# Expert projections of sorted rows: gated rows turned for two tiles at once, down projections on the two halves of the partitions

## The reference

```
xn = layernorm(x)
s  = attention(xn) @ w_out.T
expert = argmax(xn @ gate_w.T)                   # one of 8 for each of 4096 rows
inter  = relu(xn @ wg[expert])**2 * (xn @ wu[expert])   # 64 wide
g  = silu(inter @ wd[expert])                    # 256 wide
out = x + s * g
```

## Time and profile before

| | before |
|---|---|
| median of 3 runs | 1484.09 us |
| the profiled execution | 1485.04 us |
| its span | 1483.3 us |
| TensorE matmul busy | 1450.7 us |
| DVE busy | 1346.4 us |
| ACT busy | 1192.4 us |
| POOL busy | 162.1 us |
| bytes moved by DMA | 119.55 MB |

### The profile page before, as it was taken

The page is one execution under the profiler, slowest core; times in us unless marked ns, Lnnn a source line. Parts: engine busy times, 40 slices in busy tenths (PEclk is TensorE's granted clock), DMA queues, the critical chain, the costliest instruction groups (busy, mean ns, idle before and its releaser), DMA issues.

```text
span 1483.3 us, 31996 instructions
## 1 busy us (share of the span) xinstructions
PE 1450.7 (98%) x11197; PEld 652.2 (44%) x11197; DVE 1346.4 (91%) x1979; ACT 1192.4 (80%) x2381; POOL 162.1 (11%) x221
## 2 busy tenths in 40 slices
PE   7999999999999999999999999999999999999988
PEld 5555444434475433343434344434444444434326
DVE  6689999999846999999999999999999999999906
ACT  3653588888867888888888888888888888888890
POOL 5433322200001222000010000000010000000110
PEclk9999999999999999999999999999999999999999
DMA  5875244436263455333332342333323433333323
GB/s 186 277 204 137 65 84 83 76 46 125 39 188 90 80 111 99 52 48 48 48 44 41 48 99 42 46 46 48 48 44 45 97 48 41 48 48 48 69 70 117
DMA packets 79801, 119.55 MB, mean 81 GB/s; under 512 B 28962, under 2 KB 66210, under 8 KB 72738
## 3 DMA queue, kind: packets, MB, share of 16 engines
q1 hardware_dynamic: 73714, 105.82, 36.0%
q0 software_dynamic: 3072, 8.39, 2.2%
q10 hardware_dynamic: 2896, 3.62, 0.7%
HBM read 77.15 MB, written 39.71 MB: 79 GB/s over the span
## 4 chain that ended last, share of the span: by engine, by line
PE 94%; ACT 3%; DVE 1%; issue 1%; DMA 1%; SPq 0%; POOL 0%; ACTq 0%; POOLq 0%
PE ps L1243 39%; PE ps L1257 36%; PE ps L1231 5%; PE ps L1159 3%; ACT arena L658 2%; PE ps L1437 2%; PE ps L1160 1%; PE ps L1390 1%; PE ps L1374 1%; PE ps L1192 1%; PE ps L1184 1%; PE ps L1171 1%; PE ps L1341 1%; ACT x_sb L658 1%; PE ps L1136 0%
## 5 line engine op out<-in xcount | busy, mean ns | idle before, releaser
L1231 PE MATMUL ps<-ks,qs 48*128 48x512 f32 x1984 | 692.7, 444 | 0.0
L1243 PE MATMUL ps<-qs,ks 50*128 50x512 f32 x2048 | 680.6, 435 | 9.3 <-ACT x_sb L658 7.6
L809 DVE TENSOR_REDUCE arena<-ps 128x1 f32<-128x512 f32 x992 | 639.0, 681 | 16.5 <-PE ps L1231 16.2
L658 ACT ACTIVATE arena<-ps 128x512 f32<-128x512 f32 x1056 | 564.3, 605 | 86.9 <-PE ps L1243 79.7
L812 DVE TENSOR_REDUCE arena<-ps 128x1 f32<-128x1024 f32 x496 | 603.7, 1217 | 0.8 <-PE ps L1231 0.7
L658 ACT ACTIVATE x_sb<-ps 128x512 f32<-128x512 f32 x992 | 535.3, 598 | 64.9 <-PE ps L1243 44.9
L1243 PEld LDWEIGHTS ps<-qs,ks 50*128 50x128 f32 x2048 | 329.5, 184 | 485.0 <-issue 200.9
L1231 PEld LDWEIGHTS ps<-ks,qs 48*128 48x128 f32 x1984 | 325.2, 184 | 16.5 <-DVE arena L809 9.3
L1257 PE MATMUL ps<-arena 128*32 128x256 f32 (+1 forms) x3104 | 308.5, 469 | 5.5 <-ACT arena L658 4.1
L1257 PE MATMUL ps<-x_sb,arena 128*32 128x256 f32 (+1 forms) x2960 | 290.2, 464 | 0.0
L1257 PEld LDWEIGHTS ps<-arena 128*32 128x32 f32 x3104 | 62.3, 108 | 125.6 <-issue 125.6
(11 more groups left out here) (116 smaller groups left out, 623.2 us busy)
## 6 DMA issues: line engine op xcount, KB each, us to landing
qs<-parts_d SPq DMA_DIRECT2D x186, 128.0 KB
ks<-parts_d SPq DMA_DIRECT2D x186, 128.0 KB
parts_d<-arena SPq DMA_DIRECT2D x64, 256.0 KB, 2.8
xs_d<-arena SPq DMA_DIRECT2D x13, 384.0 KB, 3.5
arena<-xs_d SPq DMA_DIRECT2D x13, 384.0 KB, 3.8
ys_d<-arena SPq DMA_DIRECT2D x13, 384.0 KB, 2.8
x_sb<-in_x SPq DMA_DIRECT2D x2, 2048.0 KB, 13.1
onum_d<-arena SPq DMA_DIRECT2D x124, 32.0 KB
```

Of the source, the lines that this page charges most:

```text
L658: nc.scalar.activation(prob_of(pi, s, kb)[:, c * W:(c + 1) * W], ps[:, bank, :], ACT.Exp, scale=SCALE).then_inc(exp_done[bank], 1)
L809: nc.vector.tensor_reduce(most[head_slot][:, tile, u:u + 1], ps[:, AB + lo, :], AX.X, ALU.max).then_inc(a_reduced[u], 1)
L1231: ins = nc.tensor.matmul(ps[:, AB + c, :], qs[head_slot][ABASE:ABASE + KR, tile * P:(tile + 1) * P].bitcast(F32R), ks[head_slot][ABASE:ABA ...
L1243: nc.tensor.matmul(ps[:, bank, :], ks[s][at:at + KS, kb * P:(kb + 1) * P].bitcast(F32R), qs[s][at:at + KS, c * W:(c + 1) * W].bitcast(F32R ...
```

## The change

A step of each `experts` function now deals with a pair of tiles. The gated rows of an even tile go to columns 0 to 63 of `inter`, those of the odd tile behind it to columns 64 to 127. One turn makes both the stationary operand: the even tile on partitions 0 to 63 of `interT`, the odd tile on 64 to 127. The down projection of the even tile runs on partitions 0 to 63, that of the odd one on 64 to 127, one behind the other in TensorE's order and into banks 6 and 7. The down weights are loaded into both halves of `wd2` (four transfers, no longer two). The even tile takes them there, by the number of its expert; for the odd tile POOL copies the weights of its expert from the upper half of `wd2` to one of two fixed places in the tile `turn`, which is no longer used by then (`stage_down`). The zeroing by POOL goes. ACT does the copies and Relus of two tiles and then two Silus. SP's order of loads and stores is as before.

```diff
     NE = -(-NF // FP) * FP
+    NF2 = -(-NF // 2)
...
         res_at = at[0]
+        down_up = [turn[:, i * 8:(i + 1) * 8, :].rearrange("p t w -> p (t w)") for i in range(2)]
...
                                      src[:, k, :].rearrange("p (e f) -> p e f", f=DE)).then_inc(expert_weights, 16)
-                for i in range(2):
-                    sp.dma_start(wd2[0:DE, :, :].rearrange("p (c i) d -> p c i d", i=2)[:, :, i, :],
-                                 wd_in[i * DE:(i + 1) * DE, :, :]).then_inc(expert_weights, 16)
+                for half in range(2):
+                    for i in range(2):
+                        rows = wd2[half * DE:(half + 1) * DE, :, :].rearrange("p (c i) d -> p c i d", i=2)
+                        sp.dma_start(rows[:, :, i, :], wd_in[i * DE:(i + 1) * DE, :, :]).then_inc(expert_weights, 16)
...
                 sums_out(1, FB - 1)
-                for i in range(NF + 2):
-                    if i + 1 < NF:
-                        turned_out(i + 1)
-                    if i < NF:
-                        act.wait_ge(hid_done, i + 1)
-                        if i >= 2:
-                            act.wait_ge(inter_ready, i - 1)
-                        nc.scalar.activation(hr[i % 2], ps[:, EB + i % 2, 0:DE], ACT.Relu).then_inc(relu_done, 1)
-                    if i >= 2:
-                        act.wait_ge(y_done, i - 1)
-                        g, z = divmod(i - 2, FG)
-                        if g >= XR and z == 0:
-                            act.wait_ge(y_stored[g % XR], g // XR * 16)
-                        nc.scalar.activation(ysb[g % XR][:, z, :], ps[:, YB + i % 2, 0:D], ACT.Silu).then_inc(y_out, 1)
+                for j in range(NF2 + 2):
+                    for i in (2 * j, 2 * j + 1):
+                        if i + 1 < NF:
+                            turned_out(i + 1)
+                        if i < NF:
+                            act.wait_ge(hid_done, i + 1)
+                            if i >= 2:
+                                act.wait_ge(inter_ready, i - 1)
+                            nc.scalar.activation(hr[i % 2], ps[:, EB + i % 2, 0:DE], ACT.Relu).then_inc(relu_done, 1)
+                    for i in (2 * j - 4, 2 * j - 3):
+                        if 0 <= i < NF:
+                            act.wait_ge(y_done, i + 1)
+                            g, z = divmod(i, FG)
+                            if g >= XR and z == 0:
+                                act.wait_ge(y_stored[g % XR], g // XR * 16)
+                            nc.scalar.activation(ysb[g % XR][:, z, :], ps[:, YB + i % 2, 0:D], ACT.Silu).then_inc(y_out, 1)
...
-                for i in range(NF + 1):
-                    if i < NF:
+                for j in range(NF2 + 1):
+                    for i in (2 * j, 2 * j + 1):
+                        if i >= NF:
+                            continue
                         dve.wait_ge(relu_done, i + 1)
                         nc.vector.tensor_tensor(hu[i % 2], hr[i % 2], ps[:, EB + i % 2, DE:2 * DE], ALU.mult).then_inc(hu_ready, 1)
                         dve.wait_ge(hu_ready, i + 1)
-                        if i == 0:
-                            dve.wait_ge(pads_zeroed, 3)
-                        if i >= 2:
-                            dve.wait_ge(inter_turned, i - 1)
-                        nc.vector.tensor_tensor(inter[i % 2][:, 0:DE], hu[i % 2], hr[i % 2],
+                        if j >= 2:
+                            dve.wait_ge(inter_turned, j - 1)
+                        nc.vector.tensor_tensor(inter[j % 2][:, i % 2 * DE:(i % 2 + 1) * DE], hu[i % 2], hr[i % 2],
                                                 ALU.mult).then_inc(inter_ready, 1)
-                    if i >= 1:
-                        dve.wait_ge(inter_turned, i)
-                        if i >= 3:
-                            dve.wait_ge(y_done, i - 2)
-                        nc.vector.tensor_copy(interT[(i - 1) % 2], ps[:, PVB, 0:P]).then_inc(inter_out, 1)
+                    if j >= 1:
+                        dve.wait_ge(inter_turned, j)
+                        if j >= 3:
+                            dve.wait_ge(y_done, 2 * (j - 2))
+                        nc.vector.tensor_copy(interT[(j - 1) % 2], ps[:, PVB, 0:P]).then_inc(inter_out, 1)
...
+            def stage_down():
+
+                pool.wait_ge(expert_ready, 1)
+                pool.wait_ge(expert_weights, 16 * 8)
+                pool.wait_ge(v_staged[1], FB + 1)
+                for i in range(1, NF, 2):
+                    g, z = divmod(i, FP)
+                    if z == 1:
+                        packed = pool.value_load(expert[0:1, g:g + 1], min_val=0, max_val=E ** FP - 1)
+                    which = pool.snap(packed // E ** z % E, min_val=0, max_val=E - 1)
+                    if i >= 4:
+                        pool.wait_ge(y_done, i - 3)
+                    if i > 1:
+                        pool.wait_ge(down_staged, i // 2)
+                    nc.gpsimd.tensor_copy(down_up[i // 2 % 2][DE:P, :].unsqueeze(1),
+                                          wd2[DE:P, bass.ds(which, 1), :]).then_inc(down_staged, 1)
+
...
             pool.wait_ge(pt_out, NT)
-            nc.gpsimd.memset(wd2[DE:P, :, :], 0.0).then_inc(pads_zeroed, 1)
-            pool.wait_ge(pads_zeroed, 2)
-            for i in range(2):
-                ins = nc.gpsimd.memset(inter[i][:, DE:P], 0.0)
-            ins.then_inc(pads_zeroed, 1)
-            pool.wait_ge(pads_zeroed, 3)
             for pi in range(2, FB):
                 for s in range(2):
                     stage(0, pi, s, pi)
             for s in range(2):
                 stage(0, FB, s, FB)
+            stage_down()
...
-                pe.wait_ge(expert_weights, 16 * 6)
-                pe.wait_ge(pads_zeroed, 3)
-                for i in range(NF + 2):
-                    if i + 1 < NF:
-                        turn_sorted(i + 1)
-                    if i < NF:
-                        pe.wait_ge(xs_out, i + 1)
-                        if i >= 2:
-                            pe.wait_ge(relu_done, i - 1)
-                            pe.wait_ge(hu_ready, i - 1)
-                        for k in range(KC):
-                            last = nc.tensor.matmul(ps[:, EB + i % 2, 0:2 * DE], xsT[i % 2][:, k, :],
-                                                    wgu[:, k, bass.ds(which[i], 1), :], start=(k == 0), stop=(k == KC - 1))
-                        last.then_inc(hid_done, 1)
-                    if 1 <= i <= NF:
-                        if i == 1:
+                pe.wait_ge(expert_weights, 16 * 8)
+                for j in range(NF2 + 2):
+                    for i in (2 * j, 2 * j + 1):
+                        if i + 1 < NF:
+                            turn_sorted(i + 1)
+                        if i < NF:
+                            pe.wait_ge(xs_out, i + 1)
+                            if i >= 2:
+                                pe.wait_ge(relu_done, i - 1)
+                                pe.wait_ge(hu_ready, i - 1)
+                            for k in range(KC):
+                                last = nc.tensor.matmul(ps[:, EB + i % 2, 0:2 * DE], xsT[i % 2][:, k, :],
+                                                        wgu[:, k, bass.ds(which[i], 1), :], start=(k == 0), stop=(k == KC - 1))
+                            last.then_inc(hid_done, 1)
+                        if i + 1 < NF:
+                            expert_of(i + 1)
+                    if 1 <= j <= NF2:
+                        if j == 1:
                             pe.wait_ge(o_out[1], past(FB))
-                        pe.wait_ge(inter_ready, i)
-                        if i >= 2:
-                            pe.wait_ge(inter_out, i - 1)
-                        nc.tensor.transpose(ps[:, PVB, 0:P], inter[(i - 1) % 2], ident[:]).then_inc(inter_turned, 1)
-                    if i >= 2:
-                        if i == 2:
+                        pe.wait_ge(inter_ready, min(2 * j, NF))
+                        if j >= 2:
+                            pe.wait_ge(inter_out, j - 1)
+                        nc.tensor.transpose(ps[:, PVB, 0:P], inter[(j - 1) % 2], ident[:]).then_inc(inter_turned, 1)
+                    if j >= 2:
+                        if j == 2:
                             pe.wait_ge(a_reduced[GROUP_OF[YB - AB]], past(FB * 2 * KB + AHEAD - KB))
-                        pe.wait_ge(inter_out, i - 1)
-                        if i >= 4:
-                            pe.wait_ge(y_out, i - 3)
-                        nc.tensor.matmul(ps[:, YB + i % 2, 0:D], interT[(i - 2) % 2], wd2[:, bass.ds(which.pop(i - 2), 1), :],
-                                         start=True, stop=True).then_inc(y_done, 1)
-                    if i + 1 < NF:
-                        expert_of(i + 1)
-                pe.wait_ge(inter_out, NF)
+                        else:
+                            pe.wait_ge(y_out, 2 * (j - 2))
+                        pe.wait_ge(inter_out, j - 1)
```

(13 more changed lines are left out.)

## The result

The changed kernel takes 1497.90 us in the median of 6 runs (1491.03 to 1504.89), the kernel before 1483.74 (1482.64 to 1485.97): a ratio of 1.0087, with an interval of 1.0055 to 1.012. In a second set of runs it was 1496.92 against 1484.40, 1.0085 (1.0069 to 1.0101). It is slower by some 13 us, outside the range that was given; and its runs lie much wider apart than those of the kernel before in this set. (In larger sets that kernel has single long runs too, up to 1492.55 us at a mean clock of 0.993, where most of its runs have 0.997 or 0.998.) The profiled execution, of 1491.41 us, is one of the two shortest of its six.

The account below looks back on a forecast made before the run. It took SP's loads queued behind stores as decisive, 8.82 us per three steps, with ACT's 2.60 us a pair elsewhere. The stage ends at 458.0 instead of 456.19; 1.8 added to 1484.09 gives 1485.9 us, range 1480.5 to 1491.

Parts of the forecast that it names:

- The sum of the stage: Step times added over the experts' stage: last down pass at 458.0 instead of 456.19, 1.8 us slower.
- the clock: Rival, chance 0.20: clock halves inside the experts' stage, 0.75 us per 3.5 us stretch; seven such stretches give 1491.
- the rivals: Other cases: loads don't bind 0.17 (1481.4), clock falls 0.20 (1491), halves serial or sequencer overhead 0.12, POOL late 0.03.
- What bounds the kernel: In the experts' stage before the change, TensorE's own order sets the pace, 1.41 us a tile, and ACT follows.
- SP's chain: Loads of sorted rows queue behind stores awaiting Silus: every second group late, three steps 8.82 us; taken as decisive.
- ACT's chain: Two Silus in a row delay the copy that frees the turns' bank: 2.60 us a pair, 1.30 a tile.
- Counting the steps: Adding up ends of down passes through the experts' stage, from 405.3 to 458.0 for the last.
- Step 5: Pass 5 of TensorE's new pair loop, which waits for a load; its down passes were forecast to end at 414.65.
- step 2: Pass 2 of TensorE's new pair loop, where the count starts; about 1.1 us a tile without Silus, end at 405.3.
- The halves side by side: A pair's two down projections on TensorE run together, saving 0.38 of a possible 0.43 us a pair.
- The switch between the shapes: Row groups change TensorE's array shape twice a pair: 0.1 us a switch, counted once on the chains.
- POOL and DVE: Both have slack; POOL's 19 weight copies are wanted over 5 us later, so 1 to 2 us is covered.

Follow-up runs that it names:

- e2: The changed kernel with SP's store of each result group one group later, so loads queue behind the previous group's store: 1488.32 us, ratio 1.0038 to the kernel before.
- e8: The kernel before with SP storing each group ahead of the next load, so the load queues behind a waiting store: 1487.72 us, ratio 1.0029.
- e13: One more profile of the changed kernel, unaltered: span 1488.4 us, stage 63.3 us.
- e1: The changed kernel run again without edits: 1496.92 us, ratio 1.0085 to the kernel before; its profile has a span of 1494.7 us.
- e3: The changed kernel with filler matmuls inside the experts' stage, between hidden passes and the next turns: 1493.57 us, ratio 1.0071 to the kernel before.

## Why the prediction was wrong

It said 1485.9 us and no change that can be measured, by a stage 1.8 us longer; it was 13 us. Two steps failed. The sum of the stage came to 1.8 us, where the four profiles have 5.0 to 6.4. And the clock, which the sum put at nothing and the rivals only inside the stage, cost some 7 us behind it.

*What bounds the kernel, and SP's chain.* Right in mechanism and place: the turns of tiles 12, 18, 24, 30 and 36, and only these, wait for landings, every second group, by 1.51, 0.74, 1.55, 1.06 and 1.03 us (about 1.6 foreseen for each), and e2 and e8 show the cause by taking it away and by putting it into the kernel before. Too small in size: three steps take 433.97 - 424.33 = 9.64 us in the profile, where 8.82 was worked out. It is 1.76 from the turns to the end of the down passes (424.33 to 426.09; 1.58 was put), 2.76 for the next step (2.60), 0.84 to the load's issue (as put), and 4.28 from there to the turns (429.69 to 433.97), where 3.70 + 0.10 stood. Of these terms the landing was mis-sized most. The median of before was taken for the five that matter; the one above took, in us from issue to landing,

```profile
arena<-xs_d SPq DMA_DIRECT2D x1, 384.0 KB, 4.2
```

and the five 4.2, 4.3, 4.2, 3.7 and 3.7.

*ACT's chain.* 2.60 us a step was foreseen, 2.75 measured. Two terms were short: the second down passes start 0.32 after the first, not 0.22 (428.15 to 428.47), and from the hidden passes to the turn of gated rows it is 0.55, not 0.45 (430.15 to 430.70). At 1.38 us a tile against 1.41 before, the pairs gained nothing even without the loads, so there was nothing to set against the waits: with the loads out of the way (e2) the stage is 60.2 us, 1.9 longer than before.

*Counting the steps.* Step 5 ends at 416.01 + 0.38 = 416.39, 1.7 us after the 414.65 of the prediction, and the last down pass 4.2 after its 458.0. Of these 4.2, 1.1 are there when step 2 ends (406.4 instead of 405.3; the stage had begun 0.5 later), 2.2 come in the steps that wait for a load and those just ahead of them, and 0.9 in the others and the tail. The stage of e13, without any fall of the clock, is 5.0 longer than before: the step of the argument that gave 1.8 was right in sign and under half in size.

*The clock* had a chance of 0.20. It is the larger part of the miss. It was put inside the stage, where TensorE waits for loads, and priced at 0.75 us for 3.5 us at half clock. Of four profiles of the changed kernel one has a fall inside the stage, and three have one behind it, where the scores start and every pass counts; in e1 it lasts for 17 us. The price there is 0.36 to 0.38 us for one at half clock. The profile of before showed just that stretch, and the prediction used it as a sign of what sparse passes do but not as the place that a longer, thinner end of the stage would reach into. In the median the clock's part is some 7 us, by subtraction: 13 less the 5 to 6.4 by which the stages of the four profiles are longer than before. An estimate from the mean clocks agrees: the middle runs have 0.991 to 0.993 and the kernel before 0.998, which makes some 18 us more at half clock, and at 0.37 each 6.6 us.

*The halves side by side.* Right: they start within 0.01 us. The switch between the shapes was put at 0.1 us on one side; it is 0.09 on the way in (0.20 instead of 0.11) and 0.09 on the way out (0.31 instead of 0.22), and another 0.1 lies between the two passes of a half. The Trainium skill, TensorEngine Tiling, Key Properties, says that changing the tiling mode drains TensorE. If that meant waiting for the whole recorded turn, it would be 0.27 from the turn to the down pass; the trace has 0.20, so it agrees in that a switch costs time, and not in a wait of that length.

*POOL and DVE.* Right: POOL's copy takes 0.40 and stands two steps ahead; it waits 48.3 us in all for TensorE (L1107) and TensorE never for it.

## What to carry to other kernels

When a result is delivered later, follow what is queued behind its store: here a load of the next input stood in the same queue, lost two to three tiles of its lead, and cost 3.6 us. Before engines are made faster in a stage, ask which copy frees the bank that the next step needs; moving that copy ahead of two Silus took 4.1 us off the stage. And a stage that ends thinly just ahead of a dense one can pay at the start of the dense one, so the clock's state at the border belongs into the sum, with the spread that it brings.

## What the runs showed of the hardware

- One program, three lengths of a fall: behind the thin end of the stage the clock was at 1.2 GHz for 6.8 us in one run of the changed kernel and for 17.1 in another (after 11 passes in 3.5 us), and a third had none, though its last 3.5 us were as thin (12 passes, 2.13 us busy, as in the first). Behind the stage single profiles of this kernel differ by up to 5.6 us, nearly all from this. For each us at half clock the dense stage behind pays 0.36 to 0.38 us.
- In the first profile a store of 384 KB lands 2.8 to 3.4 us after issue and the load behind it 3.2 to 4.3; single loads of the same size take 5 and more, in both kernels, up to 5.7 in e3.
- Two float32 matmuls on partitions 0 to 63 and 64 to 127 start within 0.01 us of each other and share their time, but the two passes of each are 0.32 us apart, where a full-height one has 0.22. Of the 0.43 us that side by side could save a pair, 0.25 are left with the saved turn counted in.
